# Two-layer recurrent transformer with routed experts: rows that carry their target and gate, and one indexed write per tile in place of gathers

## The reference, cut to what matters

```python
probs = softmax(x @ router_w.T)                      # 8 experts
token_probs, probs_idx = top_k(probs, 2)             # two experts and gates a token
gates = sum(token_probs[..., None] * one_hot(probs_idx, 8), axis=-2)
for each expert e:
    y = gelu(x @ wg_e.T + wg_b_e)
    h = y * (x @ w1_e.T + w1_b_e)
    acc += (h @ w2_e.T + w2_b_e) * gates[..., e]
```

## Time and profile before

| | |
|---|---|
| median of 3 runs | 647.43 us (644.2 to 652.0) |
| the profiled execution's own time | 646.75 us |
| its span in the profile | 644.9 us |
| mean granted clock of TensorE | 0.934 of full |
| busy: PE, DVE, ACT, POOL | 559.0, 384.6, 267.8, 205.3 us |
| DMA traffic | 72.03 MB, 112 GB/s over the span |

### The profile page before, as it was taken

How to read it: one execution, slowest core, us unless ns; L and a number is a source line. 1 busy time by engine, 2 the same in 40 slices (tenths; PEclk the granted TensorE clock), 3 DMA queues, 4 the chain that set the end, 5 groups by cost and what they waited for, 6 DMA issues and landing times. The chain is left out here.

```text
span 644.9 us, 13192 instructions
## 1 busy us (share of the span) xinstructions
PE 559.0 (87%) x3235; PEld 410.7 (64%) x3236; DVE 384.6 (60%) x1141; ACT 267.8 (42%) x775; POOL 205.3 (32%) x254
## 2 busy tenths in 40 slices
PE   7987998885299999999999988589797888879986
PEld 4854666564199999999999966444344343443442
DVE  6898887664044444444444456476676866657733
ACT  4353554552144555445544545435233242323411
POOL 6300456666300000000000026464745647374100
PEclk9599999998589999999999999789988989798988
DMA  9910542111168888778878711000101011010000
GB/s 297 308 64 22 176 170 87 57 62 41 41 185 232 233 234 234 233 236 235 236 230 235 206 33 35 16 13 20 49 2 49 12 37 41 8 49 0 16 17 16
DMA packets 56010, 72.03 MB, mean 112 GB/s; under 512 B 7056, under 2 KB 42800, under 8 KB 55728
## 3 DMA queue, kind: packets, MB, share of 16 engines
q1 hardware_dynamic: 41664, 58.67, 30.6%
q0 software_dynamic: 4096, 8.40, 4.2%
q10 hardware_dynamic: 10224, 4.66, 2.5%
HBM read 54.01 MB, written 15.60 MB: 108 GB/s over the span
## 5 line engine op out<-in xcount | busy, mean ns | idle before, releaser
L1132 DVE SCALAR_TENSOR_TENSOR AR<-bank,B1T,AR 128x128 f32<-128x128 f32 x284 | 80.0, 345 | 108.5 <-ACT AR L1482 103.3
L1482 ACT ACTIVATE AR<-bank,BGT 128x128 f32<-128x128 f32 x284 | 80.9, 368 | 59.5 <-PE bank L726 59.5
L472 POOL DMA_INDIRECT XN<-slots_y,SLOT x32 | 32.4, 1014 | 219.5 <-DMA slots_y<-YO 209.0
L455 POOL DMA_INDIRECT slots_x<-XN,SLOT x64 | 62.0, 969 | 84.9 <-DVE TEXP L1017 41.2
L726 PE MATMUL bank<-AR,WGE 128*128 128x128 f32 x568 | 77.1, 280 | 0.2 <-ACT AR L1475 0.2
L734 PE MATMUL bank<-AR,WGE 128*128 128x128 f32 x568 | 75.9, 277 | 0.0
L743 PE MATMUL bank<-W2E,AR 128*128 x568 | 75.1, 275 | 0.5 <-DVE AR L1132 0.5
L726 PEld LDWEIGHTS bank<-AR,WGE 128*128 128x128 f32 x568 | 70.7, 196 | 0.9 <-issue 0.6
L734 PEld LDWEIGHTS bank<-AR,WGE 128*128 128x128 f32 x568 | 70.0, 194 | 0.0
L743 PEld LDWEIGHTS bank<-W2E,AR 128*128 128x128 f32 x568 | 69.1, 192 | 0.7 <-issue 0.7
L636 PE MATMUL bank<-AR 128*128 128x128 f32 x320 | 49.2, 286 | 20.5 <-ACT AR L1401 19.4
(11 more groups left out here) (180 smaller groups left out, 950.4 us busy)
## 6 DMA issues: line engine op xcount, KB each, us to landing
WGE<-in_wgu SPq DMA_DIRECT2D x71, 512.0 KB, 5.1
XG<-slots_x ACTq DMA_DIRECT2D x71, 64.0 KB, 4.6
slots_y<-YO SPq DMA_DIRECT2D x71, 64.0 KB, 4.2
slots_x<-W1E SPq DMA_DIRECT2D x7, 576.0 KB, 6.6
X<-in_x SPq DMA_DIRECT2D x8, 256.0 KB, 4.7
AR<-XNT SPq DMA_DIRECT2D x8, 256.0 KB
W2E<-in_w SPq DMA_DIRECT2D x1, 2048.0 KB
out<-X SPq DMA_DIRECT2D x8, 256.0 KB
```

The costliest lines, as they stand in the source:

```text
L455: pool.indirect_dma_start(out=slots_x, out_offset=bass.IndirectOffsetOnAxis(ap=SLOT[:, k, n:n + 1], axis=0), in_=XN[:, n, :], in_offset=No ...
L472: pool.indirect_dma_start(out=y[:, n, :], out_offset=None, in_=slots_y, in_offset=bass.IndirectOffsetOnAxis(ap=SLOT[:, k, n:n + 1], axis=0 ...
L1132: s = dve.scalar_tensor_tensor(out=HT[u][:, c, :], in0=B[3 + u][:, c * P:(c + 1) * P], scalar=B1T[:, bass.ds(e, 1), c], in1=ZB[u][:, c, :] ...
L1482: act.activation(ZB[u][:, c, :], B[1 + u][:, c * P:(c + 1) * P], ACT.Gelu, bias=BGT[:, bass.ds(e, 1), c]).then_inc(c_gelu, 1)
```

## The change

Routed rows get two more columns. `XR` holds each token tile with 130 columns: 128 features, the row number in token order at which the result belongs (choice k, token t: k * 4096 + t), and the gate. The row numbers come from the host with the constants (`TAG`); VectorE writes the gates beside them and copies the tags of choice 0 behind all rows (part 1 of `route`), and POOL replaces them by those of choice 1, four tiles at a time, in the course of the indexed writes, which now go choice by choice for groups of four tiles. Unused rows of `slots_x` get row numbers beyond the tokens (`PAD`), so that every row of a tile has a target of its own.

In the expert stage `XG` has four buffers of 130 columns. POOL copies the two tag columns to `DST` (as integers) and `GSL` (`c_tags`), VectorE adds the bias into `YB` and multiplies by the gate into `YO` with a second instruction, and POOL, not SP, writes `YO` with one indexed DMA to `rows_y` in token order (`c_send`). The last layer has no gathers: SP reads 16 plain blocks of 256 KB into `Y0` and `Y1`, and POOL adds the two (`both`). `d_front1` is gone on ScalarE and VectorE; the early tanh and gate of sequence 1 move to the end of sequence 6 and the start of sequence 7.

```diff
-        XN = sb("XN", [P, NT, P])
+        XR = sb("XR", [P, NT, ROW])            # ROW = P + 2
+        XN = XR[:, :, 0:P]
-        XG = [sb(f"XG{u}", [P, P])[:] for u in range(2)]
+        XG = [sb(f"XG{q}", [P, ROW]) for q in range(WBUFS)]
+        DST = [sb(f"DST{q}", [P, 1], U32) for q in range(WBUFS)]
+        GSL = [sb(f"GSL{q}", [P, 1]) for q in range(WBUFS)]
+        YB = [sb(f"YB{u}", [P, P]) for u in range(2)]
...
 SP, expert stage and after
-            def store_slots(j, u):
-                sp.dma_start(slots_y_t[:, bass.ds(j, 1), :], YO[u][:, None, :]).then_inc(c_st[u], 16)
...
             for u in range(2):
                 sp.wait_ge(c_st[u], 16 * stores(u))
+            for b in range(NSEQ):
+                for k, y in ((0, Y0), (1, Y1)):
+                    sp.dma_start(y[:, b * TPS:(b + 1) * TPS, :], rows_y_t[:, k, b * TPS:(b + 1) * TPS, :]
+                                 ).then_inc(d_gat[b], 16)
+            for b in range(NSEQ):
+                sp.wait_ge(d_gat[b], 16 * 2)
+                sp.sem_inc(d_got, 1)
...
 POOL, routed writes
-            for n in range(NT):
-                for k in range(2):
-                    if 2 * n + k and (2 * n + k) % SCAT_BURST == 0:
-                        pool.wait_ge(scat, 16 * (2 * n + k))
...
+            for group in range(0, NT // SCAT_BURST, 2):
+                send_rows(0, group)
+                landed()
+                send_rows(0, group + 1)
+                second_tags(group)
+                landed()
+                pool.wait_ge(tagged, group + 2)
+                send_rows(1, group)
+                second_tags(group + 1)
+                landed()
+                pool.wait_ge(tagged, group + 3)
+                send_rows(1, group + 1)
+                landed()
...
 POOL, expert stage
+            def c_tags(j, q):
+                pool.wait_ge(c_ld[q], (j - q) * 4 + 16)
+                if j >= WBUFS:
+                    pool.wait_ge(c_yo, j - (WBUFS - 1))
+                    pool.wait_ge(c_st[q % 2], (j - q % 2) * 8 - 16)
+                pool.tensor_copy(DST[q][:], XG[q][:, P:P + 1])
+                pool.tensor_copy(GSL[q][:], XG[q][:, P + 1:P + 2]).then_inc(c_tag, 1)
+
+            def c_send(j, q):
+                pool.wait_ge(c_yo, j + 1)
+                pool.wait_ge(c_tag, j + 1)
+                pool.indirect_dma_start(
+                    out=rows_y, out_offset=bass.IndirectOffsetOnAxis(ap=DST[q][:, 0:1], axis=0),
+                    in_=YO[q % 2][:], in_offset=None).then_inc(c_st[q % 2], 16)
+
+            def c_step(j, q, last=False):
+                if not last:
+                    c_tags(j + 2, (q + 2) % WBUFS)
+                c_send(j, q)
...
 POOL, last layer
+            def both(b):
+                tiles = slice(b * TPS, (b + 1) * TPS)
+                pool.wait_ge(d_got, b + 1)
+                pool.tensor_tensor(Y0[:, tiles, :], Y0[:, tiles, :], Y1[:, tiles, :], ALU.add).then_inc(d_mo, 1)
...
                 if b + 3 < NSEQ:
-                    gather(b + 3)
+                    both(b + 3)
...
 VectorE, routing and expert stage
+                    link(dve.tensor_tensor(GATE[1], DIF, GATE[0], ALU.mult))
+                    dve.wait_ge(a_xn2, NSEQ)
+                    dve.wait_ge(a_tr, NSEQ)
+                    dve.tensor_copy(XR[:, :, P:], TAG[:, 0, :, :]).then_inc(tagged, 1)
...
-            def c_out(j, u, e):
+            def c_out(j, q, e):
+                u = q % 2
                 dve.wait_ge(c_y, j + 1)
+                dve.tensor_tensor(YB[u][:, None, :], B[5 + u][:, None, 0:P], B2E[:, bass.ds(e, 1), :], ALU.add
+                                  ).then_inc(c_sum, 1)
                 if not (isinstance(j, int) and j < 2):
                     dve.wait_ge(c_st[u], (j - u) * 8)
-                dve.tensor_tensor(YO[u][:, None, :], B[5 + u][:, None, 0:P], B2E[:, bass.ds(e, 1), :], ALU.add
-                                  ).then_inc(c_yo, 1)
+                dve.wait_ge(c_tag, j + 1)
+                dve.wait_ge(c_sum, j + 1)
+                dve.tensor_scalar(YO[u][:], YB[u][:], GSL[q][:, 0:1], None, ALU.mult).then_inc(c_yo, 1)
...
 ScalarE, expert stage
                     if load:
-                        load_slots(j + 3, 1 - u)
+                        if not (isinstance(j, int) and j < 1):
+                            act.wait_ge(c_tag, j)
+                        load_slots(j + 3, (q + 3) % WBUFS)
```

More of the change, by code:

```diff
@@ L123, in build @@
         NMR = sb("NMR", [P, NT])
-        GATE = sb("GATE", [P, 2, NT])
+        TAG = CST[:, C_TAG:C_TAG + 4 * NT].rearrange("p (k n c) -> p k n c", k=2, n=NT)
+        GATE = [TAG[:, k, :, 1] for k in range(2)]
         SLOT = sb("SLOT", [P, 2, NT], U32)
@@ L174, in build @@
         CNT = r1.take(2, NT * E)
-        ZERO = r1.take(9 * P)
+        ZERO = r1.take(FILL, ROW)
         rb = Region()
@@ L283, in build @@
         o_done = sem("o_done")
-        c_ld = [sem("c_ld0"), sem("c_ld1")]
+        c_ld = [sem(f"c_ld{q}") for q in range(WBUFS)]
+        c_tag = sem("c_tag")
+        c_sum = sem("c_sum")
         w_ld = [sem(f"w_ld{q}") for q in range(WBUFS)]
@@ L461, in _ @@
             pool.tensor_tensor(TAPW[:, PAD - LOCAL, :], TAPW[:, PAD - LOCAL, :], CHN[:, 0, :], ALU.add).then_inc(w_ready, 1)
[L464 to L474 removed]
+            def c_tags(j, q):
[15 more added lines that the diff above has]
+                c_send(j, q)
+            c_tags(0, 0)
+            c_tags(1, 1)
+            for j in range(SLOT_TILES):
+                c_step(j, j % WBUFS, last=j + 2 >= SLOT_TILES)
+            pool.wait_ge(c_y, SLOT_TILES)
             own = [0]
@@ L515, in _ @@
             pool.memset(ZERO1, 0.0).then_inc(d_zero, 1)
-            gather(0, 2, TPS)
-            gathered(0)
-            gather(1, 0, 2)
-            pool.wait_ge(d_gat[1], 16 * TPS)
+            both(0)
+            both(1)
             front(0)
-            gather(1, 2, TPS)
-            gathered(1)
             scales(0)
@@ L526, in _ @@
             update(0)
-            gather(2)
+            both(2)
             for b in range(NSEQ):
@@ L1465, in _ @@
             act.wait_ge(scat, 16 * 2 * NT)
-            for u in range(2):
-                load_slots(u, u)
+            for j in range(3):
+                load_slots(j, j)
             finish(NB - 1)
@@ L1485, in _, with c_step @@
             e_next, e_this = (act.alloc_register(f"act_expert_{n}") for n in ("next", "this"))
-            def c_step(j, u, last=False, load=True):
+            def c_step(j, q, last=False, load=True):
+                u = q % 2
                 e = act.snap(e_this, min_val=0, max_val=E - 1)
```

176 lines of the change are left out of this document (74 added, 102 removed).

## The result

| | before | changed |
|---|---|---|
| median | 647.88 us of 4 runs (644.2 to 652.0) | 627.53 us of 4 runs (625.4 to 633.4) |
| ratio to before, 95% interval | | 0.9698 (0.961 to 0.9786) |
| profiled execution, its span | 646.75, 644.9 us | 627.03, 624.8 us |
| mean granted clock of TensorE | 0.934 | 0.947 |

The change makes the kernel 3.0% faster. The forecast of 621.0 us was 6.5 us too low, inside its range of 609 to 636. Cut at the marks that the prediction used, the two profiles differ as follows. The last columns come from more profiles of kernels whose code in that stretch is the same (two of before; the changed kernel, its repetition and those experiments that leave the stretch alone).

What follows compares the result with a forecast made beforehand. POOL's serial routed writes, the expert stage's tiles and gathers delaying attention and the last layer were taken as bounds. 0.7 + 1.6 + 0.4 - 6.0 - 1.3 - 19.7 - 1.5 = -25.8 from 646.75 gave 621.0 us, range 609 to 636.

Steps and rivals of the forecast that it cites:

- the likeliest case: Whole kernel: the forecast of 621.0 us holds, own bounds about 613 to 629; chance 0.60.
- the store's cycle: Expert stage: POOL's wait for store j - 2 paces tiles, 639 to 666 us; chance 0.06 plus 0.04.
- Start, +0.7 forecast: Before routed writes: small copies on POOL and VectorE, 0.25 us each, and 0.2 for more constants.
- Routed writes, +1.6 forecast: POOL's indexed writes: 520-byte rows cost 0.1 us in each of 16 groups; tag copies cost nothing.
- Expert stage, +0.4 forecast: End of expert stage: TensorE waits for VectorE's added second instruction, 0.28 us and a semaphore.
- L: Expert stage: time from POOL's store issue to landing, taken as 3.5 us; up to 5.0 costs nothing.
- Attention, -7.3 forecast with the first `d_roots`: Attention on sequences 6 and 7: -6.0 us from gather waits and scaling removed; first `d_roots` -1.3.
- The claim on the loads: Sixteen plain loads after the last store: sequences 0 and 1 arrive before ScalarE gets to their tanh.
- Last layer, steps 0 to 4: Five last-layer steps without POOL's gathers: 23.6 us each, 118.0 for 137.7, so -19.7 us.
- the base: Last-layer step without gathers: 23.2 us, the middle of 22.9 and 23.5 from two steps.
- The -0.4 for eight removed products: Each last-layer step: four products removed on ScalarE and four on VectorE save 0.4 us.
- `both` beside `d_front3`, +0.8: Each last-layer step: POOL's added sum beside VectorE's chain work costs 0.8 us, bounds 0 and 1.27.

Runs made afterwards that it cites:

- experiment 3: Kernel before, with the last layer's gathers on POOL replaced by sixteen plain loads on SyncE, gate products kept, no `both`: 622.0 us, ratio 0.9563.
- experiment 4: Changed kernel with 512-byte rows in `slots_x` and its loads, tag copies still made, targets and gates from constants: 629.8 us, ratio 0.9689.
- experiment 8: Changed kernel with `both` behind `rms` and waiting for its own loads, `d_front2(0)` at k = 1, third load behind `finish`: 617.44 us, ratio 0.9516.
- experiment 6: Changed kernel with tag copies also waiting for the landing of the previous tile's store, so one store in flight: 701.2 us in one run.
- experiment 5: Changed kernel with VectorE's `d_front2(0)` moved from k = 2 to k = 1 of attention on sequence 7: 624.9 us in one run.
- experiment 1: Changed kernel with POOL's `both` moved from behind `scales` to behind the power `rms`: 627.68 us, ratio 0.9646.

## Why the prediction came out as it did

**The sign, the order of the terms and the likeliest case** were right: experiment 3 shows that taking eight gathers a sequence off POOL is enough for the whole gain, and the store's cycle did not pace the expert stage. The 6.5 us that were missing are, in this pair, mainly 3.3 us of the steps, 2.2 of the start and 1.5 of the routed writes; the start's are chance, since it moves by 5 us from run to run, and so is a part of the attention's 0.8 us the other way. Of the prediction's own signs, TensorE at full clock and no release of the steps' `d_roots` by POOL came true; the steps were to take 23 to 24 us, and `d_front3` starting a microsecond late, its sign of being wrong, nearly came true with 0.86.

**Start, +0.7 forecast.** Not measurable: the start varies by 5 us with the granted clock in both kernels. The zero fill, which the prediction left out, nearly doubled its time to landing, but the start does not show it: 63.5 us with it in the changed kernel's second profile, 63.4 without it before.

**Routed writes, +1.6 forecast, +1.6 in the means.** The means are those of the nine profiles with 520-byte and the four with 512-byte rows. The copies are free, the rows cost 0.05 to 0.14 us in each of 16 groups; the rest is scatter. By the Trainium skill (DMA: Bandwidth & Descriptors, How a descriptor splits into AXI transactions) a transaction reads at most 256 bytes and starts on a 256-byte boundary. The rows of `slots_x` start at multiples of 520 bytes, so at most 248 bytes behind such a boundary, and by this rule each takes three transactions, never the four that the prediction also counted, where one of 512 takes two: 1.5 times, an estimate from that section. ScalarE's loads, which read such rows, don't show it: their queue kept the engines for 2.7% of the span (2.6% with 512-byte rows, experiment 4). Nor does an indexed write; only the zero fill, which writes such rows while the engines are full, is slower in that order: 12.9 us for 7.0, and 184 GB/s for 298 from 22 to 30 us.

**Missed: +0.5** for the third load, whose issue stands ahead of `finish` on ScalarE. The prediction had no term for it; experiment 8, with that load behind `finish`, is back at 5.1 us.

**Expert stage, +0.4 forecast, 0.0 measured.** The wait that the 0.4 stands for is there: from the end of the last down product to the first product of attention it is 0.91 us for 0.49, and the rest of the stage, which differs by 2 us and more between profiles, hid it. The threshold (5.0; 4.8 measured) was right. L was mis-sized, 4.4 for 3.5: here the row of the direct store, 4.2, was the better witness than the packet counts. It cost nothing only because 4.4 is still below 4.8. But L also stood at 2.3 for long stretches of other profiles at the same pace (experiment 6), and no run shows what packet counts have to do with either; 3.5 is between two values, and measured in neither.

**Attention, -7.3 forecast with the first `d_roots`, -4.5 to -8.1 measured.** Named rightly: `scales(0)` is late next. Its start was mis-sized: the forecast moved it to VectorE's statistics as they stood in the trace, and experiment 5 shows that these stood too late by their place in VectorE's order. The claim on the loads was near for the data (3.8 and 7.4 us for 3.2 and 4.9, still ahead of the tanh) and wrong for the count behind them.

**Last layer, steps 0 to 4: the term that was off most.** 23.6 us a step forecast, 24.25 measured, 3.3 us in five. Its parts: (1) the base, 23.2 for a step without gathers. Experiment 3 gives 23.3, and 23.5 without its first step. The lower of the two steps averaged, that from 441.43 us, was not typical: its `scales` happened to start clear of VectorE's work, with 0.23 us for the first instruction, where the later steps show 0.63 or 1.70. (2) The -0.4 for eight removed products: nothing to be seen (117.2 us for five steps in experiment 1, without them, 116.5 in experiment 3, with them). (3) `both` beside `d_front3`, +0.8: 0.82 measured, by moving it. The Trainium skill's rule (SBUF, Who interferes with whom) says that one of the two instructions waits for the whole of the other, and by it the prediction had -17.6 us for these steps; its own terms, 1.27 us in place of 0.8 in each of five, make -17.3. The trace agrees in kind: `both` runs from 503.28 to 504.54, and VectorE's instruction, which the profile starts at 503.42, ends at 504.63, just behind it. What is lost is 0.86 us, neither all of 1.27 nor the 1.12 that `both` still had to run at 503.42. That -17.3 is nearer to the measured -16.4 than -19.7 owes to the errors of the other two parts.

**Step 5, -1.5 forecast, -1.7 measured** in this pair; the second profile of before has 23.7 us there, so most of it was that trace's clock.

## What to carry to other kernels

When work is taken off an engine, look again at the place of what stays: a sum of 1.3 us, put beside the one VectorE instruction that the chain needed, cost 4 us of 20, and one line of VectorE's that stood a place too late another 2.6, seen in one profile. A step without the disturbance, taken as the base of a forecast, should be one of several, and one reads in it whether its small instructions happened to fall in a gap. And a term smaller than what the clock moves, here 5 us at the start, is settled by marks of the same stretch in several profiles, not by two totals.

## What the runs showed of the hardware

- TensorE's granted clock falls from 1.0 to 0.5 between 10.6 and 13.6 us in all thirteen profiles and comes back between 25.9 and 41.9 us, differently from run to run of the same code (1.0 is its level of 2.4 GHz, 0.5 that of 1.2); in four of them it falls once more at 33 to 35 us. The first routed write follows it, from 63.4 to 68.6 us. Seven more products ahead of the first transposes gained nothing.
- The time from an indexed store's issue to its landing is no constant of a kernel: beside weights every 2.79 us it was 4.2 us for one part of the expert stage and 2.3 us for the next, in one execution; with one store in flight and weights every 3.7 us it was 2.9.
- Sixteen plain loads of 256 KB issued in a row take SyncE 13 us: the first issue lasts 0.38 us, later ones 0.5 to 2.2. Anything behind them in that queue waits.
- POOL and VectorE hold each other up in both directions: VectorE lost 0.86 us behind `both`, and POOL's small instruction took 0.64 us for 0.23 behind a product of VectorE.
